# Attention maxima in a macaron block on one Trainium2 core: four single PSUM banks of scores become two pairs of banks

## The reference

```python
x = x + 0.5 * ffn(layernorm(x), ...)        # 8 experts, top 2 of each token, 3 layers with relu
x = x + attn(layernorm(x), w_qkv, w_out)
x = x + 0.5 * ffn(layernorm(x), ...)

def attn(x, w_qkv, w_out):                  # 16 heads of 16 features, 4096 tokens, causal
    q, k, v = split(x @ w_qkv.T)
    logits = q @ k.T / 4                    # [head, query, key]
    probs = softmax(where(tril, logits, -inf))
    return (probs @ v) @ w_out.T
```

## Time and profile before

| | |
|---|---|
| time, median of 3 runs | 2191.81 us (2191.78 to 2194.29) |
| the profiled execution, its span | 2202.7 us |
| PE busy | 2120.6 us, 96% |
| DVE busy | 1848.5 us, 84% |
| ACT busy | 1624.4 us, 74% |
| POOL busy | 515.3 us, 23% |

### The profile page before, as it was taken

How to read it: one execution, slowest core, us unless ns; L and a number is a source line. 1 busy time by engine, 2 the same in 40 slices (tenths; PEclk the granted TensorE clock), 3 DMA queues, 4 the chain that set the end, 5 groups by cost and what they waited for, 6 DMA issues and landing times.

```text
span 2202.7 us, 97616 instructions
## 1 busy us (share of the span) xinstructions
PE 2120.6 (96%) x42439; PEld 1851.5 (84%) x42443; DVE 1848.5 (84%) x3894; ACT 1624.4 (74%) x3567; POOL 515.3 (23%) x1295
## 2 busy tenths in 40 slices
PE   5999989999999999999999999999999999969998
PEld 3788865599999999999999999998999997748885
DVE  7666666999999999999999999999999995666665
ACT  5344456688888888888888888888888888334442
POOL 1333213413122131221212213122121211023330
PEclk8899999999999999999999999999999999969998
DMA  8211114301010010100101001010010100331112
GB/s 276 64 45 48 35 38 141 96 19 33 4 32 22 16 33 4 32 23 13 33 4 33 23 13 32 4 33 24 12 33 4 32 4 6 113 106 46 49 48 84
DMA packets 94853, 94.32 MB, mean 43 GB/s; under 512 B 41108, under 2 KB 83864, under 8 KB 94424
## 3 DMA queue, kind: packets, MB, share of 16 engines
q0 software_dynamic: 41376, 42.91, 7.6%
q1 hardware_dynamic: 52704, 45.15, 6.4%
q10 hardware_dynamic: 344, 0.01, 0.0%
HBM read 62.24 MB, written 25.43 MB: 40 GB/s over the span
## 4 chain that ended last, share of the span: by engine, by line
PE 91%; DVE 5%; ACT 1%; issue 1%; DMA 1%; another core or an unknown queue 0%; POOL 0%; DVEq 0%; ACTq 0%; SPq 0%
PE bank L1233 44%; PE bank L1225 19%; PE bank L1109 17%; PE bank L1175 2%; PE bank L1271 2%; PE bank L1187 1%; PE bank L1120 1%; PE bank L1336 1%; DVE stats L1366 1%; PE bank L1127 1%; PE bank L1279 1%; PE bank L994 1%; DVE x_res L1686 0%; DVE rows L1388 0%; DVE work L1555 0%
## 5 line engine op out<-in xcount | busy, mean ns | idle before, releaser
L1233 PE MATMUL bank<-work 96*32 96x512 bf16 (+4 forms) x17920 | 1415.8, 363 | 2.9 <-DVE work L1725 2.5
L926 ACT ACTIVATE feat<-bank 128x512 f32<-128x512 f32 (+3 forms) x2304 | 1250.9, 565 | 156.4 <-PE bank L1233 78.7
L1725 DVE TENSOR_REDUCE work<-bank 128x1 f32<-128x512 f32 (+3 forms) x2176 | 1299.7, 639 | 64.7 <-PE bank L1233 53.0
L1225 PE MATMUL bank<-feat,phase 128*17 128x128 f32 x16896 | 1140.2, 272 | 2.3 <-issue 2.3
L1225 PEld LDWEIGHTS bank<-feat,phase 128*17 128x17 f32 x16896 | 831.6, 98 | 67.2 <-issue 2.9
L1233 PEld LDWEIGHTS bank<-work 96*32 96x32 bf16 (+1 forms) x17920 | 810.2, 96 | 69.1 <-DVE work L1725 10.8
L1109 PE MATMUL bank<-work 128*128 128x256 f32 (+1 forms) x1872 | 398.3, 363 | 0.5
L1109 PEld LDWEIGHTS bank<-work 128*128 128x128 f32 x1872 | 325.5, 192 | 36.6 <-DVE work L1617 0.8
L601 POOL TENSOR_SCALAR_AFFINE_SELECT feat<-feat 128x128 f32<-128x128 f32 x512 | 146.3, 293 | 447.4 <-ACT feat L926 442.7
L543 POOL DMA_INDIRECT work<-token_table,row_no x142 | 138.0, 972 | 302.7 <-PE bank L1120 149.5
L1617 DVE COPY work<-phase 128x514 f32 x234 | 101.2, 435 | 121.9 <-ACT work L840 97.0
(11 more groups left out here) (195 smaller groups left out, 1392.8 us busy)
## 6 DMA issues: line engine op xcount, KB each, us to landing
phase<-in_w SPq DMA_DIRECT2D x12, 1024.0 KB, 12.2
work<-qk_parts POOLq DMA_DIRECT2D x60, 192.0 KB, 3.7
token_table<-rows SPq DMA_DIRECT2D x8, 1056.0 KB, 8.7
qk_parts<-phase SPq DMA_DIRECT2D x20, 384.0 KB, 2.8
work<-qk_parts POOLq DMA_DIRECT2D x60, 128.0 KB, 4.2
qk_parts<-work SPq DMA_DIRECT2D x12, 384.0 KB, 2.6
x_res<-in_x SPq DMA_DIRECT2D x8, 512.0 KB, 7.6
work<-work SPq DMA_DIRECT2D x256, 1.0 KB
```

The lines of the kernel that those rows point to most:

```text
L926: eng.activation(p_ring[:, n % P_RING, lo:QB], s_bank("probs", n)[:, lo:QB], ACT.Exp, scale=HD ** -0.5).then_inc(sig.s_done, 1)
L1225: mm = eng.matmul(bank[ACC_BANK][GRID * g:GRID * g + VW, 0:P], v_aug[:, t, h, :], p_ring[:, n % P_RING, g * P:(g + 1) * P], start=(t == 0) ...
L1233: mm = eng.matmul(out[GRID * g:GRID * (g + 1), width], left[:, GRID * g:GRID * (g + 1)], right, start=start, stop=stop)
L1725: eng.tensor_reduce(maxima[:, h % 2, j, i, k + 1:k + 2], scores[:, 0:hi - lo], AX_X, ALU.max).then_inc(sig.a_done, 1)
```

## The change

Banks 3 and 4, and banks 6 and 7, become two tensors of 1024 columns. Two neighbouring key blocks of one row (k even and k odd) are written into the two halves of one pair, and DVE reduces both with one instruction of up to 1024 elements. A diagonal item, a row's last block when their number is odd, and a row of one block stand in a pair alone. PE signals `a_full` once for a pair, and before the first item of pair p it waits until DVE has reduced pair p - 2. `maxima` has 5 instead of 9 columns for a row, so `unit_max` reads 20 instead of 36 elements. PE's matmuls and the step list stay the same.

```diff
-A_BANKS = (3, 4, 6, 7)
+A_PAIRS = ((3, 4), (6, 7))
...
-SLOTS = 1 + NJ
+A_PAIR, A_LAST, A_TOTAL = [], [], 0
+for _n, (_h, _j, _i, _k) in enumerate(A_ITEMS):
+    _last = _n + 1 == len(A_ITEMS) or _k % 2 == 1 or A_ITEMS[_n + 1][1:3] != (_j, _i)
+    A_PAIR.append(A_TOTAL)
+    A_LAST.append(_last)
+    A_TOTAL += _last
+SLOTS = 1 + NJ // 2
...
-                        out = bank[A_BANKS[n % len(A_BANKS)]]
+                        out = bank[A_PAIRS[A_PAIR[n] % len(A_PAIRS)][k % 2]]
                         stack_ready(h, j)
-                        need.wait_ge(sig.a_done, n - len(A_BANKS) + 1)
+                        need.wait_ge(sig.a_done, A_PAIR[n] - len(A_PAIRS) + 1)
...
-                        mm.then_inc(sig.a_full, 1)
+                        if A_LAST[n]:
+                            mm.then_inc(sig.a_full, 1)
...
                     elif what == "scores":
+                        if not A_LAST[n]:
+                            continue
                         h, j, i, k = A_ITEMS[n]
                         lo, hi = keys_of(j, i, k)
-                        scores = bank[A_BANKS[n % len(A_BANKS)]]
-                        need.wait_ge(sig.a_full, n + 1)
+                        scores = pair[A_PAIR[n] % len(A_PAIRS)]
+                        need.wait_ge(sig.a_full, A_PAIR[n] + 1)
...
-                            eng.tensor_reduce(maxima[:, h % 2, j, i, k + 1:k + 2], scores[:, 0:hi - lo], AX_X,
-                                              ALU.max).then_inc(sig.a_done, 1)
+                            eng.tensor_reduce(maxima[:, h % 2, j, i, k // 2 + 1:k // 2 + 2],
+                                              scores[:, 0:k % 2 * QB + hi - lo], AX_X, ALU.max).then_inc(sig.a_done, 1)
```

More of the change, by code:

```diff
@@ L323, in macaron_block @@
         gate_b_col = sb("gate_b_col", [P, 1])
-        bank = [ctx.enter_context(nc.psum_tensor(f"bank{i}", [P, QB], F32)) for i in range(8)]
+        single = {i: ctx.enter_context(nc.psum_tensor(f"bank{i}", [P, QB], F32)) for i in (0, 1, 2)}
+        pair = [ctx.enter_context(nc.psum_tensor("pair0", [P, 2 * QB], F32))]
+        single[ACC_BANK] = ctx.enter_context(nc.psum_tensor(f"bank{ACC_BANK}", [P, QB], F32))
+        pair += [ctx.enter_context(nc.psum_tensor("pair1", [P, 2 * QB], F32))]
+        bank = [single[i] if i in single else pair[i // 6][:, (i - A_PAIRS[i // 6][0]) * QB:
+                                                          (i - A_PAIRS[i // 6][0] + 1) * QB] for i in range(8)]
         table = [nc.dram_tensor(f"token_table{f}", (S + 1, ROW), F32).ap() for f in range(2)]
@@ L1313, in transpose_heads @@
             def transpose_heads(n):
-                need.wait_ge(sig.a_done, len(A_ITEMS))
+                need.wait_ge(sig.a_done, A_TOTAL)
                 need.wait_ge(sig.divided, len(UNITS))
@@ L1767, in last_scores @@
     for n, (h, j, i, k) in enumerate(A_ITEMS):
-        last[h * NJ + j] = n
+        last[h * NJ + j] = A_PAIR[n]
     return last
```

## The result

The changed kernel takes 2393.4 us (median of 4 runs, 2392.47 to 2396.64) against 2191.8 us (median of 4, 2190.09 to 2194.29): a ratio of 1.0922, 95% interval 1.0907 to 1.0937, or +201.6 us. The forecast was +221, 2413 us. The profiled execution has a span of 2391.9 us.

A forecast was written before the change was run, and what follows sets the result against it. PE was taken as the bound, DVE 9% below it. PE's waits for pairs, 13.5 us a head or 216 us in 16 heads, plus 5 us made +221 us on 2191.8: 2413 us, range 2340 to 2490.

The forecast's parts named there:

- 0.52 us until DVE starts: Time from the start of a group on PE until DVE starts its reduce, taken as the middle of 0.45 and 0.60.
- DVE adds no queue of its own in these places.: Where PE waits for a pair, DVE was to be free for its reduce, having 78 us of work a head.
- The places: Points in a head's step list where PE waits for a pair: some 25 waits of 0.54 us, 13.5 us a head.
- narrow item alone: Next pair holds one narrow item (j = 2, 4, 6, rows 1 to 3): 9 places, wait 0.88, 7.9 us a head.
- single 512: Next pair holds one 512 item (row 0 of j = 3, 5, 7): 3 places, wait 0.53, 1.6 us a head.
- row ends of 640 and 768: Next pair is 512 + 128 or + 256 (j = 3, 5, 7): 6 places, wait 0.32, 1.9 us a head.
- the pair of 896: Pair of 896, then the diagonal, then row 0: 4 places, wait 0.25, 1.0 us a head.
- start of a head: Units j = 0 and 1, with pairs of one narrow item: 0.75 us a head.
- full pair to full pair: Between two full pairs, a wait only where pv pauses and a step is 0.44: 0.25 us a head.
- the list's work was 1.2% too long: PE work summed from the step list, 92.2 us a head against 91.1 in the trace; added 0.35 us a head, 5 us.
- R: Time from the start of a pair's last item until PE may write the pair two later: 1.79 us for 1024 elements.
- W: PE work the step list puts from a pair's last item to the first item two pairs later; 1.97 us between full pairs.

The follow-up runs named there:

- joins_where_spare: Kernel before, four banks in turn, two neighbouring items of a row reduced together only where the next two items are 512 wide (608 joins); 2209.0 us, ratio 1.0038.
- joins_but_last_row: Kernel before, four banks in turn, joins only before two 512-wide items and none in a head's last row (576 joins); 2195.26 us, ratio 1.0019.
- two_banks: Kernel before with two single banks (3, 6) instead of four for the scores of pass A, nothing joined; 2310.04 us, ratio 1.0543.

## Why the prediction was right

The mechanism, the direction and the size hold. By steps:

- **PE is the bound, by the waits and not by busy time.** Right. The three runs that lighten DVE without holding a place too long (joins_where_spare and its two variants) gain nothing.
- **The reduce is linear, 1.22 us; way back 0.056.** Measured 1224 ns and 0.06. The Trainium skill ("Advanced Engine Details and Errata", TRN2 Errata) advises tiles of 512 or 1024 elements to keep the overhead small, and says that one instruction may read several PSUM banks. Both hold here: two joined reduces of 512 take 1.22 us of DVE where one by one they take 0.60 + 0.69 = 1.29, 0.07 us saved for a join. Neither matters off the path.
- **0.52 us until DVE starts.** Near the middle, but it isn't one number. Where the four matmuls of a block start together it is 0.44, as in the example above and for a lone group. Where they start one after the other it is longer, though DVE stands ready. From the timeline of head 6, PE, DVE and PE's weight load:

```profile
1044.84 0.39 PE L1244 MATMUL pair<-work 96*32 96x512 bf16 x2
1045.06 0.38 PE L1244 MATMUL pair<-work 96*32 96x512 bf16 x1
1045.23 0.42 PE L1244 MATMUL pair<-work 96*32 96x384 bf16 x3
...
1045.69 1.22 DVE L1739 TENSOR_REDUCE work<-pair 128x1 f32<-128x1024 f32 x1 [0.63 <-PE pair L1244]
...
1046.97 0.10 PEld L1282 LDWEIGHTS pair<-work 96*32 96x32 bf16 x4 [1.21 <-DVE work L1739]
```

The block's first matmul starts at 1044.84; its fourth, at 1045.27, is in the merged third row. DVE has been idle for 0.63 us when it starts at 1045.69: 0.85 after the first matmul, 0.42 after the fourth. Over the 23 waits a head of more than 0.15 us, in ten middle heads of the trace, DVE starts 0.39 to 1.01 us after the first matmul of the block, 0.51 in the median and 0.59 in the mean, and 0.44 in the mean after the fourth.
- **"DVE adds no queue of its own in these places."** Right but for one place: in those heads DVE is still at work on an earlier reduce in 1 of the 23, behind the diagonal item at the start of a head, which costs 0.3 us there.
- **The places.** Per head, at every pair the distance from the last matmul before to the first of the pair, less 0.1 us of pace, where at least 0.1 us is left: narrow item alone 7.5 us (forecast 7.9), single 512 1.5 (1.6), before row ends of 640 and 768 1.6 (1.9), behind the pair of 896 0.7 (1.0), start of a head 0.8 (0.75), full pair to full pair 0.6 (0.25): 12.7 against 13.5, with heads at 12.6. In the last of these the blocks stand where pv pauses, and their matmuls are spread out: DVE starts 0.82 us after the first. The 20 us by which the sum is too high are thus the 0.35 us a head added because the list's work was 1.2% too long (5 us), and places that were 0.9 us a head too dear (13.5 against heads of 12.6, some 14 us), with full pair to full pair alone too cheap. That the errors of the places partly cancel is luck. How much of each lies in R and how much in W isn't separated: matmuls that are spread out make DVE start later, and they also let PE run out of work later.
- **max_row.** Costed at nothing, right for the changed kernel, where its weight load waits for POOL twice in the whole execution, 4.2 us. The same step cost some 0.4 us a head in joins_where_spare, where the other waits were gone.
- **What would show it.** 768 reduces at 1.22: yes. DVE's share near 80%: yes. Heads of 104.6: 103.7. Idle time of 150 to 250 us put down to DVE's line: on the weight loads 183 us from 600 to 1900 us, and half of that on the matmuls.
- **The clock.** It stayed at 1.00 in the windows from 700 to 2000 us, through waits of up to 1.2 us.
- **The rule on rotation.** The Trainium skill ("Perfetto Trace Analysis", Matmuls) wants independent groups to rotate through different PSUM banks so that the evacuation of one overlaps the next one's matmuls. The runs agree and put numbers beside it: three single banks cost 9 us against four, two 119, and two pairs that are held long 202.

Left open: the 4 us of joins_but_last_row, and 7 of the 15 us by which two_banks lies above its expected middle. All the counts made with 0.44 us came out low, by 5 to 15 us where a loss was large (57 twice for 51, 119 for 104, 222 for 217, 55 for 42, this one in part by `max_row`), as they would if DVE starts later than that in part of the waits; no run tests this alone.

## What to carry to other kernels

Before making one instruction out of two on an engine that is not the bound, add up how long the buffer is then held (fill, start, instruction, way back) and compare it with the work that the bound engine has before it wants that buffer again, at the irregular places above all: narrow items, lone items, steps without their usual work. Grouping buffers in pairs also makes every lone item take two; keep the ring by single buffer and join only where the next items are long, and nearly all of the cost goes (202 us became 4 to 8 here), though an engine with time to spare still brings no gain. Check the second chain too: a later reduce moves everything that waits for the last one.

## What the runs showed of the hardware

- A reduce of 1024 float32 over two neighbouring PSUM banks takes 1224 ns, and one of 512 within a bank 687: 537 ns for the second half, at 134 ns for each 128, as from 128 to 512 within one bank (283 to 687). No cost of crossing the boundary shows.
- DVE, when it is free, starts its reduce some 0.43 us after the last of the four matmuls of a block has started, whether the four start together (0.43 at 1073.45) or spread over 0.43 us (0.42 at 1045.27).
- PE starts 0.056 us after the end of the reduce that it waits for, in the kernels before and after.
- With 12% fewer matmuls in the same time, after waits of up to 1.2 us, the granted clock stayed at 1.00 in the windows from 700 to 2000 us, and PE's busy time still read 92%.
